# Reordering the interleaved zone of a two-layer gated cross-attention kernel

## The reference

```python
x = x + tanh(g_xattn[0]) * L0_xattn(layernorm(x), ctx, mask)
x = x + tanh(g_ffn[0])   * L0_ffn(layernorm(x))
x = x + tanh(g_xattn[1]) * L1_xattn(layernorm(x), ctx, mask)
x = x + tanh(g_ffn[1])   * L1_ffn(layernorm(x))
```

## Time and profile before

| | |
|---|---|
| median of 3 runs | 1417.22 us (1417.06 to 1417.59) |
| profiled execution | 1417.42 us, its span 1415.6 us |
| busy: PE, DVE, ACT, POOL | 1363.1, 961.2, 862.4, 628.2 us |
| granted TensorE clock, mean | 0.991 of full |
| ACT_TABLE_LOAD | 16 at silu (L601), 16 at exp (L681), 1283 ns each |
| chain that ended last | PE 75%, issue 10%, POOL 6%, DVE 4%, ACT 3% |

### The profile page before, as it was taken

The page is one execution under the profiler, slowest core; times in us unless marked ns, Lnnn a source line. Parts: engine busy times, 40 slices in busy tenths (PEclk is TensorE's granted clock), DMA queues, the critical chain, the costliest instruction groups (busy, mean ns, idle before and its releaser), DMA issues.

```text
span 1415.6 us, 25935 instructions
## 1 busy us (share of the span) xinstructions
PE 1363.1 (96%) x7924; PEld 1139.9 (81%) x7924; DVE 961.2 (68%) x1965; ACT 862.4 (61%) x3287; POOL 628.2 (44%) x670
## 2 busy tenths in 40 slices
PE   5999999999999999999989999899999999999997
PEld 4788888888888888766666688788888888888886
DVE  4678788787878797776666767555555555555665
ACT  3656666566666666666666765566666656665541
POOL 2536657565657585334445233333342333232232
PEclk9999999999999999999999999999999999999999
DMA  7011120112111110010100011201001010100001
GB/s 276 1 46 53 42 69 24 61 46 63 52 57 52 63 48 19 1 46 30 46 31 1 1 30 46 82 31 46 30 11 63 0 44 30 44 30 0 1 16 45
DMA packets 33701, 59.39 MB, mean 42 GB/s; under 512 B 2784, under 2 KB 25952, under 8 KB 29536
## 3 DMA queue, kind: packets, MB, share of 16 engines
q1 hardware_dynamic: 33632, 58.54, 12.5%
HBM read 56.43 MB, written 2.10 MB: 41 GB/s over the span
## 4 chain that ended last, share of the span: by engine, by line
PE 75%; issue 10%; POOL 6%; DVE 4%; ACT 3%; DMA 1%; SPq 0%; POOLq 0%; ACTq 0%; DVEq 0%
PE bank L1028 51%; PE bank L1020 7%; PE bank L1106 7%; PE bank L1157 5%; PE bank L1167 2%; POOL rstd L501 2%; POOL w_lo L469 1%; PE bank L1037 1%; ACT probs L681 1%; PE bank L1148 1%; ACT f_s L601 1%; POOL ln_rstd L491 1%; ACT L681 1%; POOL x_sb L570 1%; PE bank L1179 1%
## 5 line engine op out<-in xcount | busy, mean ns | idle before, releaser
L469 POOL TENSOR_TENSOR w_lo<-w_raw,w_hi (+1 forms) x150 | 229.2, 1544 | 200.2 <-ACT w_hi L612 199.4
L642 ACT ACTIVATE squares<-bank 128x128 bf16<-128x128 f32 x512 | 134.3, 277 | 259.8 <-PE bank L1028 259.8
L923 DVE SCALAR_TENSOR_TENSOR probs<-bank,mask_sb 128x512 f32<-128x512 f32 x128 | 88.2, 689 | 234.0 <-PE bank L1106 234.0
L681 ACT ACTIVATE probs<-probs,negmax 128x128 f32<-128x128 f32 x512 | 198.8, 391 | 4.9 <-DVE negmax L927 4.5
L497 POOL TENSOR_TENSOR meansq<-sumsq,scalars 128x5 f32<-128x5 f32 x128 | 28.6, 224 | 325.2 <-ACT squares L642 325.2
L501 POOL TENSOR_TENSOR rstd<-meansq,scalars 128x5 f32<-128x5 f32 x128 | 153.1, 1196 | 10.8 <-POOL meansq L497 1.1
L1028 PE MATMUL bank<-w_hi,oT_hi 128*128 (+1 forms) x512 | 150.7, 416 | 0.0
L1028 PE MATMUL bank<-w_hi,xT_hi 128*128 (+1 forms) x512 | 142.4, 400 | 0.6 <-DVE w_lo L753 0.6
L1028 PE MATMUL bank<-w_hi,xT_lo 128*128 (+1 forms) x512 | 138.2, 392 | 0.0
L1028 PE MATMUL bank<-w_lo,oT_hi 128*128 (+1 forms) x512 | 138.2, 392 | 0.0
L1028 PE MATMUL bank<-w_lo,xT_hi 128*128 (+1 forms) x512 | 137.9, 391 | 0.0
(11 more groups left out here) (132 smaller groups left out, 3074.6 us busy)
## 6 DMA issues: line engine op xcount, KB each, us to landing
w_raw<-in_wq SPq DMA_DIRECT2D x16, 1024.0 KB, 4.9
w_raw<-in_wo SPq DMA_DIRECT2D x16, 1024.0 KB, 4.7
fw_raw<-in_ffn_w SPq DMA_DIRECT2D x36, 192.0 KB, 2.3
w_raw<-in_wk SPq DMA_DIRECT2D x16, 256.0 KB, 5.3
w_raw<-in_wv SPq DMA_DIRECT2D x16, 256.0 KB, 5.5
x_sb<-in_x SPq DMA_DIRECT2D x4, 512.0 KB, 9.9
ctx_raw<-in_ctxT SPq DMA_DIRECT2D x4, 512.0 KB, 10.5
out<-x_sb SPq DMA_DIRECT2D x8, 256.0 KB, 2.0
```

The lines of the kernel that those rows point to most:

```text
L469: last = nc.gpsimd.tensor_tensor(lo, raw, hi.bitcast(FP32), ALU.subtract)
L642: last = nc.scalar.activation(squares[:, h // 2, (b + 1) % 4, h % 2, :], psQ[:, h * P:(h + 1) * P], ACT.Square, scale=SCALE, accum_out=sum ...
L681: last = nc.scalar.activation(probs[:, h * P:(h + 1) * P], probs[:, h * P:(h + 1) * P], ACT.Exp, bias=negmax[:, h:h + 1], accum_out=rowsum ...
L923: nc.vector.scalar_tensor_tensor(heads(probs[:, :]), heads(psSQ[:, :]), SCALE, mask_sb[:, :].unsqueeze(1).to_broadcast([P, REP, P]), ALU.m ...
```

## The change

- ScalarE, odd steps: exp of the unit before runs ahead of silu 0, and silu 1 moves behind the kT and qT copies. Before: silu 0, kn, exp, silu 1.
- TensorE, odd steps: `gate_up(1)` moves from behind the output product to behind the value product. The i0 transposes move to the even step, behind `gate_up(2)`, and their copy behind silu 2.
- VectorE, odd steps: `pT_lo` moves ahead of qn, `hidden(0)` behind the output accumulation.
- GpSimd: it applies the norms of the FFN and of the next layer, which VectorE did; `unit_rstd` goes ahead of the FFN norm's `ln_rstd_of`. The next layer's norm is applied at the end of the accumulating odd step, a step earlier.
- Splits: steps 13, 15, 17, 19 and 21 each split two pieces early and two late; the even steps 14 to 20 split none. The zone is eight steps longer (0 to 39), and steps 29 to 39 split the pieces of the groups after.
- SyncE loads the group for steps 40 and on ahead of its wait for the folded int4 weights.
- int4: eight parts in steps 27 to 34, and one folding product in each of steps 35 to 38.

```diff
-ZONE0, ZONE1 = UNITS - 2 * BATCHES, UNITS + 2 * BATCHES
+ZONE0, ZONE1 = UNITS - 2 * BATCHES, UNITS + 3 * BATCHES
...
-              13: ((C, 0), (C, 1)), 14: ((C, 2), (C, 3)), 15: ((C, 4), (C, 5)), 16: ((C, 6), (C, 7)),
-              17: ((C, 8), (C, 9)), 18: ((E, 0), (E, 1), (E, 2)), 19: ((E, 3), (E, 4), (E, 5)),
-              20: ((E, 6), (E, 7)), 21: ((E, 8), (E, 9)),
-              29: ((E + 1, 0), (E + 1, 1)), 30: ((E + 1, 2), (E + 1, 3)), 31: ((E + 1, 4), (E + 1, 5))}
-SPLIT_ZONE_LATE = {31: ((E + 1, 6), (E + 1, 7), (E + 1, 8), (E + 1, 9))}
+              13: ((C, 0), (C, 1)), 15: ((C, 4), (C, 5)), 17: ((C, 8), (C, 9)), 19: ((E, 2), (E, 3)), 21: ((E, 6), (E, 7)),
+              29: ((E + 1, 0), (E + 1, 1)), 30: ((E + 1, 2), (E + 1, 3)), 31: ((E + 1, 4), (E + 1, 5)),
+              32: ((E + 1, 6), (E + 1, 7)), 33: ((E + 1, 8), (E + 1, 9), (E + 2, 0)), 34: ((E + 2, 1), (E + 2, 2)),
+              35: ((E + 2, 3),), 36: ((E + 2, 4), (E + 2, 5)), 37: ((E + 2, 6),), 38: ((E + 2, 7), (E + 2, 8)),
+              39: ((E + 2, 9),)}
+SPLIT_ZONE_LATE = {13: ((C, 2), (C, 3)), 15: ((C, 6), (C, 7)), 17: ((E, 0), (E, 1)), 19: ((E, 4), (E, 5)),
+                   21: ((E, 8), (E, 9))}
...
 # SyncE
             load_group(E, 0, None, step_of(C, BATCHES - 1) + 1)
+            load_group(E + 1, 1)
             sp.wait_ge(wp_ps, KT)
...
 # GpSimd, step
                 split_lower(split_pieces(n, b, kind, j))
+                if has(n, 0):
+                    unit_rstd(n)
                 if t.norm is not None:
                     ln_rstd_of(NORM["ffn", t.norm])
-                if has(n, 0):
-                    unit_rstd(n)
+                    if t.down is not None:
+                        pool.wait_ge(clipped, SIX[2, t.down] + 1)
+                    normalise(NORM["ffn", t.norm], t.norm, f_s[:, :])
+                split_lower(late_pieces(n, kind))
+                if t.acc is not None:
+                    pool.wait_ge(qk_ps, n + 1)
+                    normalise(NORM["next", t.acc], t.acc, qn[:, :])
...
 # ScalarE, step
-                if t.down is None:
-                    split_upper(split_pieces(n, b, kind, j))
+                split_upper(split_pieces(n, b, kind, j))
...
                 if t.down is not None:
                     silu(2, t.down)
-                    split_upper(split_pieces(n, b, kind, j))
+                    act.wait_ge(i0_ps, t.down + 1)
+                    wait(act, d_ps, t.down)
+                    nc.scalar.activation(f_iqT[:, 0:4, :], by_k(psC_bf[:, 0:D]), ACT.Copy).then_inc(i0_sb, 1)
+                split_upper(late_pieces(n, kind))
...
-                if t.gate is not None:
-                    silu(0, t.gate)
...
+                if has(n, 1) and t.gate is not None:
+                    softmax_exp(n)
                 if has(n, 0):
...
-                if t.gate is not None:
-                    silu(1, t.gate)
+                if has(n, 1) and t.gate is None:
+                    softmax_exp(n)
+                if t.gate is not None:
+                    silu(0, t.gate)
...
                     nc.scalar.activation(qT[:, :], psSQ[:, :], ACT.Copy).then_inc(qT_sb, 1)
                 if t.gate is not None:
-                    act.wait_ge(i0_ps, t.gate + 1)
-                    wait(act, d_ps, t.gate)
-                    nc.scalar.activation(f_iqT[:, 0:4, :], by_k(psC_bf[:, 0:D]), ACT.Copy).then_inc(i0_sb, 1)
+                    silu(1, t.gate)
...
 # VectorE, step
-                if t.gate is not None:
-                    hidden(0, t.gate)
-                if has(n, 2):
+                if has(n, 2) and t.gate is None:
+                    probs_lower(n)
...
                 if t.gate is not None:
+                    hidden(0, t.gate)
                     hidden(1, t.gate)
```

More of the change, by code:

```diff
@@ L70, in zone_order @@
 def zone_order():
-    a, b, c, d = (UNITS // BATCHES + k for k in (-2, -1, 0, 1))
+    a, b, c, d, last = (UNITS // BATCHES + k for k in (-2, -1, 0, 1, 2))
     order = [(a, i) for i in range(4)]
@@ L79, in zone_order @@
         order += [(d, i), (c, i + 4)]
-    return order + [(d, i) for i in range(4, 8)]
+    return order + [(d, i) for i in range(4, 8)] + [(last, i) for i in range(8)]
 ZONE_ORDER = zone_order()
@@ L337, in gathered @@
         def gathered(n, kind):
-            at = n - INT4_0 - 3
-            return range(2 * at, 2 * at + 2) if kind == ZONE and 0 <= at < KT // 2 else ()
+            at = n - INT4_0 - INT4_PARTS
+            return (at,) if kind == ZONE and 0 <= at < KT else ()
         def quant_piece(q, b):
@@ L601, in silu, with softmax_exp @@
                 nc.scalar.activation(f_s[:, 0:width], psA[:, 0:width], ACT.Silu, scale=1 / FP6_UNIT).then_inc(silu_done, 1)
+            def softmax_exp(n):
+                act.wait_ge(nm_done, n)
+                for h in range(REP):
+                    last = nc.scalar.activation(probs[:, h * P:(h + 1) * P], probs[:, h * P:(h + 1) * P],
+                                                ACT.Exp, bias=negmax[:, h:h + 1], accum_out=rowsum[:, h:h + 1])
+                last.then_inc(exp_done, 1)
             def split_upper(pieces):
@@ L676, in step @@
                     nc.scalar.activation(kn[:, :], psKV[:, 0:P], ACT.Copy, scale=rstd[:, REP:REP + 1]).then_inc(kn_done, 1)
-                if has(n, 1):
-                    act.wait_ge(nm_done, n)
-                    for h in range(REP):
-                        last = nc.scalar.activation(probs[:, h * P:(h + 1) * P], probs[:, h * P:(h + 1) * P],
-                                                    ACT.Exp, bias=negmax[:, h:h + 1], accum_out=rowsum[:, h:h + 1])
-                    last.then_inc(exp_done, 1)
+                if has(n, 1) and t.gate is None:
+                    softmax_exp(n)
                 if t.gate is not None:
-                    silu(1, t.gate)
+                    silu(0, t.gate)
                 if has(n, 0):
@@ L832, in hidden, with probs_lower @@
                 quantise6(f_s[:, 0:width], c, i)
+            def probs_lower(n):
+                dve.wait_ge(pt_hid, n - 1)
+                nc.vector.tensor_tensor(pT_lo[:, :], psPO[:, :], pT_hi[:, :].bitcast(FP32),
+                                        ALU.subtract).then_inc(pt_lod, 1)
             def int4_weights(part):
-                t = part // 2
                 if part == 0:
@@ L906, in step @@
                     normalise(t.first, t.first, f_s[:, :])
-                if t.next is not None:
-                    dve.wait_ge(qk_ps, n)
-                    normalise(NORM["next", t.next], t.next, qn[:, :])
                 if t.last is not None:
@@ L928, in step @@
                                             negate=True).then_inc(nm_done, 1)
-                if t.norm is not None:
-                    if t.down is not None:
-                        dve.wait_ge(clipped, SIX[2, t.down] + 1)
-                    normalise(NORM["ffn", t.norm], t.norm, f_s[:, :])
+                if has(n, 2) and t.gate is not None:
+                    probs_lower(n)
                 if has(n, 0):
@@ L975, in step @@
                     ctx_lower(b // 2 + 1)
-                if kind == ZONE and 0 <= n - INT4_0 < 4:
+                if kind == ZONE and 0 <= n - INT4_0 < INT4_PARTS:
                     int4_weights(n - INT4_0)
@@ L1063, in step @@
                     gate_up(2, t.down)
+                    pe.wait_ge(six_done, SIX[0, t.down] + 1)
+                    transposes(f_iq[:, 0, :], psC_bf, ident_bf[:, :]).then_inc(i0_ps, 1)
                 if has(n, 0):
@@ L1141, in step @@
                                    lambda a, h: weights(3, WO0 + h * D, D)[a]).then_inc(y_ps, 1)
-                if t.gate is not None:
-                    gate_up(1, t.gate)
                 if has(n, 0):
@@ L1159, in step @@
                 if t.gate is not None:
-                    pe.wait_ge(six_done, SIX[0, t.gate] + 1)
-                    transposes(f_iq[:, 0, :], psC_bf, ident_bf[:, :]).then_inc(i0_ps, 1)
+                    gate_up(1, t.gate)
                 if t.down is not None:
```

51 lines of the change are left out of this document (30 added, 21 removed).

## The result

The changed kernel takes **1395.55 us** (median of 4 runs, 1393.14 to 1396.29) against 1417.14 for the kernel before (4 runs, 1414.59 to 1417.59): ratio 0.985, interval 0.9838 to 0.9862, so 1.5% faster. The forecast was 1394, with a range of 1386 to 1406. The profiled execution took 1396.21 us, its span is 1393.9.

The account below looks back on a forecast made before the run. Plain steps are bound by TensorE at 9.53 us, the FFN tile zone by a chain of waits across engines. From 1417.42 us, -15.2 (splits) - 1.6 (order) - 6.9 (int4) = -23.7 gives 1393.7, say 1394 us, range 1386 to 1406.

Parts of the forecast that it names:

- The splits: Even steps 14 to 20: without weight pieces, four slow pairs fall to 30.11 us, saving 15.2 us; odd steps hide them.
- The rival that the late weights hold ScalarE: Odd steps' front: splits wait for late weight loads five times, about 4 us each, so no measurable change; 3%.
- int4: Steps before 32: eight parts remove 6.9 us of waits for VectorE's unpacking and copies; folding products' 7.4 us stay.
- The order: Tiles of the zone: new engine order gains 0.2 us a tile, 1.6 us over eight tiles.
- the waits of 0.50 and 0.19 us: Even step, TensorE waiting for scaled keys and qn; both were to go because unit_rstd runs 1.6 us earlier.
- Silu 1 later by 0.38: Odd step, ScalarE: exp first delays silu 0 by 1.70 us and silu 1, with all behind it, by 0.38 us.
- the rival of the costly order: Tiles: later silu 0 and VectorE operations stretched by GpSimd add 0.5 to 1.5 us each, 1399 to 1408 us; 13%.
- The clock: TensorE's granted clock in the zone's pairs: 1.00 in all, the slow down products gone with the splits.
- The rival of a fall behind gate_up's idle time: Tiles: a 0.6 us idle stretch before gate_up 1 lowers the clock, 13.6 us come back, 1408 us; 5%.
- The norm: Norms moved to GpSimd: 1.3 us each, hidden in idle time, so 0 cost; VectorE's saving is off the path.
- the one from the slack: Even step: GpSimd's norm costs 0 up to 3.2 us, the time left before VectorE's quantisation must pass.
- the rival that ends slower: GpSimd's slow norm holds rstd and silu 0, taking the whole gain from 6.2 us on; 1432 us at 8; 6%.

Follow-up runs that it names:

- e6: Kernel before with only the weight pieces moved to odd steps, two early and two late, all else as before: 1402.42 us, ratio 0.9903.
- e2: Changed kernel with four int4 parts and two folding products a step again: 1402.21 us, ratio 0.9896.
- e3: Changed kernel with ScalarE's odd step again silu 0, scaled keys, exp, silu 1; VectorE's order stays new: 1398.21 us, ratio 0.9875.
- e5: Changed kernel with GpSimd applying the FFN's norm twice, with the same result: 1399.49 us, a single run.
- e1: Changed kernel with the weight pieces back in even steps 14, 16, 18 and 20: 1402.33 us, ratio 0.9905.
- e8: Changed kernel with the even step's last seven TensorE transposes moved behind the output product, ScalarE's order following: 1389.9 us, a single run.
- e11: e9 with the next layer's norm written to its own buffer, applied right behind unit_rstd, ahead of the late pieces: 1387.19 us, ratio 0.9796.
- e9: Changed kernel with e8's even step, and odd steps with silu 0, hidden(0), gate_up(1) and silu 1 earlier: 1391.76 us, ratio 0.9824.
- e10: Changed kernel with pieces back in even steps and the FFN norm's small steps again ahead of unit_rstd: 1405.51 us, a single run.

## Why the prediction was right, step by step

- **The splits: -15.2, measured -14.9.** The price was read as the difference of pairs with and without pieces, and e6 shows it for this edit alone. That odd steps hide the two more pieces at 0 is shown too: 29.91 with them and 29.92 without. The rival that the late weights hold ScalarE did not come.
- **int4: -6.9, measured -7.0.** e2 gives 6.9 back. Splitting the steps over 9.53 into the products' 7.4 and the waits' 7.0 was right, and every part fits in its step.
- **The order: -1.6, measured 0.** This is the term that missed, and it is 1.6 of the 1.9 us by which the zone's sum of -16.8 is off; the other 0.3 lies in the splits. Its mechanism held in the middle pairs: the waits of 0.50 and 0.19 us went, silu 1 came late, and a pair gained 0.24 us where 0.2 was forecast. But I multiplied by eight. The first and the last pair of before took 28.97 and 29.39 us, less than the pair in my window, and the new order brought them up to the same 29.9. I took one pair for all instead of summing all eight. That the total still came within 2 us rests on the two large terms.
- **Silu 1 later by 0.38: measured 0.52** (8.72 us behind the scores instead of 8.20). The hidden values started 1.60 later against 1.70, silu 1 stood 0.04 instead of 0.11 us behind the quantisation, and one operation took 0.47 instead of 0.17 us: -0.10 - 0.07 + 0.30, which is the missing 0.14 within 0.01. So the stretching that I named in the rival of the costly order came, in one operation of this chain. Beside this stands an error of reading: I took before's third table load to have waited for the quantisation's end (783.55); it waited for exp, whose last read ends at 783.64. e3 shows the load running ahead of the quantisation's end. So a load saved there is worth about 0.5 us, not the 1.3 that the prediction reads from the rows, and e3 measures 0.46 a pair. The sum was not hurt, since it took the start of silu 1 from the quantisation's end and nothing from the load.
- **The clock.** Forecast at 1.00 in all tiles; so it is. The rival of a fall behind gate_up's idle time (0.36 and 0.74 us now) did not come.
- **The norm: 1.3 us taken, 2.08 measured**, and free all the same in the middle tiles. Of the two bounds, the one from the slack decided, and it was itself low: e5 hides 4.2 us. So the rival that ends slower was farther off there than I said. The first tile has no such slack: a second norm costs it 3.7 us (e5), which the prediction did not see, since it priced all eight tiles alike.
- **Gains overlap.** I added -15.2 and -1.6 as if they were independent. With the new order in place, the splits cost only 6.1 us in even steps (e1), against 14.9 with the old (e6). The sum came out right because I priced the splits from pairs of before and the order from a pair without splits. With the pieces in even steps the order alone takes the four pairs from 135.6 to 125.7 us (e1), 9.9 less; had I added that to the -15, the same gain would have been counted twice.

Open: why the first and the last pair get longer was not tried. They had less to gain: step 9 has no accumulation and step 24 no norm, so before's step 24 took 14.14 us against 14.86 in step 22, and after it takes the same 16.2 as the others. In step 9 the 0.60 us wait behind GpSimd's norm adds to it. The 0.3 us by which step 9 begins later is less than such starts differ among runs.

## What to carry to other kernels

An edit's worth is its worth given the others: undoing one part of a change (e1: 6 us) and doing it alone (e6: 15 us) answer different questions, and a sum must take each term from rows that already have the others. Price a change from all the stretches it touches, the cheap ones at the ends too. When an engine must wait for a chain across engines, put its independent work ahead of the wait (e8), and keep long GpSimd work away from the time in which VectorE does small operations of that chain (e11).

## What the runs showed of the hardware

- A VectorE TENSOR_SCALAR on 128x16 takes 0.17 us, but 0.47 or 0.99 us when a 512-wide GpSimd instruction is running as it begins, and then ends with that instruction, within 0.03 us (the changed kernel, e9); with the instruction elsewhere it takes 0.17 again (e11). In the zone of the changed kernel this holds for all 15 such operations of 96 that begin beside a 512-wide GpSimd instruction, and for none of the other 81. The kernel before has it too: 8 operations of 0.30 to 0.36 us, beside the scaling of the probabilities. Some wide operations were not held (the multiplication from a PSUM bank at 767.07 took 0.69 us beside the norm, as without it). VectorE's own norm was, and this is the spread of the earlier trace rows: the seven of 1.02 us all began beside GpSimd's last scaling, the one of 0.54 us beside nothing. In step 20 of the kernel before:

```profile
758.48 0.78 POOL L527 TENSOR_TENSOR f_iq<-f_iq,blk_pow 128x352 bf16<-128x352 bf16 x1 [1.33 <-DVE f_iq L823]
758.52 1.02 DVE L741 TENSOR_SCALAR qn<-x_sb,ln_mv,ln_rstd 128x512 f32<-128x512 f32 x1
```

  The Trainium skill (GPSIMD Engine Reference, Specifications) says that the SBUF interfaces are shared with VectorE, with contention for VectorE instructions in a 2-port mode or with two SBUF inputs. The traces agree in that some operations are held and others are not; what it costs here is up to 0.8 us for one small operation.
- GpSimd's subtract-and-multiply by two values per partition takes 2.08 us for 128x512 in float32, against 1.28 for an add of two tensors of that size.
- A function table's load is 1.28 us and starts when ScalarE comes free, ahead of the data that its activation waits for (e3: 769.95 against 770.77). The Trainium skill (ScalarE: Activation LUTs, What ACT_TABLE_LOAD costs) puts a drain of 1.38 us beside the load; in the changed kernel the activation starts 1.29 us after the load's start (765.15 to 766.44), with no drain to be seen.
- A wait of TensorE of 1.87 us was followed by a granted clock of 0.59, which is partly the level of 1.2 GHz, one of 2.70 by 0.62 (e10, step 18) and one of 2.07 with 0.60 behind it by 0.81 and 0.71 (e5, step 9), but waits of 0.53 and 1.81 (e1) and of 1.44 us (e10) by 1.00. 1.81 and 1.87 lie too near each other for the wait's length alone to decide; what else does was not tried.
